# A displaced 5x5 convolution behind a group norm: group sums as four lane tiles inside the first stage, one lane evicted by VectorE, matrices written in place

## The chip, the cores and the metric

One NeuronCore of a Trainium2 chip runs the kernel. The metric is the device time of one execution in microseconds (us), as the median of several runs. The engines are TensorE (PE; its weight loads are shown apart as PEld), VectorE (DVE), ScalarE (ACT), GpSimd (POOL) and SyncE (SP, which here only issues loads).

## The reference, cut to what matters

```python
x = x + conv(displace(group_norm(x)))      # x: (32, 384, 64, 64) float32

def group_norm(v, G=32, eps=1e-5):         # 12 channels of one image are a group
    return (g - mean(g)) / sqrt(var(g) + eps)

def conv(x, offset):                       # 48 positions, 8 channels each
    off_round = round(offset); sub = offset - off_round
    disp = displace(x, off_round)          # whole shifts per position, zeros shifted in
    d = field + sub                        # field: 5 x 5
    kernel = exp(-sum(d * d) / 0.5); kernel /= sum(kernel)   # one 5 x 5 kernel per position
    return depthwise_conv(disp, kernel)    # 384 channels
```

The 5x5 kernel is a product of a vertical and a horizontal Gaussian, so that shift and convolution of one channel are a product with a 64x64 matrix along the rows (`ay`) and one along the columns (`ax`).

## The kernel before

**Steps.** The channels are cut into 16 superblocks of 24 channels (3 positions each); within a superblock the 32 images are 16 steps of 2 images. There are 256 steps, named `t = 16 * c + s`; two steps are a pair, and there are 128 pairs. A step's data is a tile of 128 partitions by 6 x 256 numbers, 768 KB: the partitions are 4 lanes (channels) of 32, each of them 16 row blocks by 2 images. `xin` has 16 slots, one for each step of a superblock. Loads are issued by SyncE, two DMAs a step, as soon as the slot's store has landed; stores are issued by ScalarE, two DMAs a step, 2 steps behind (`BEHIND`, line 562).

**TensorE** (lines 592 to 674) goes through a loop whose body is one pair of steps (`two_steps`). Each step has a first stage, the y products (`y_product`, L604): 48 matmuls with 32 rows and 128 columns of weights (`norm`) and 128 moving columns (`ay`), four lanes side by side, into 4 PSUM banks; and a second stage, the x products (`x_products`, L615): 48 matmuls of 64 x 64 with 64 moving columns (`ax`), in the order of positions 2, 0, 1. In float32 every matmul is two weight loads and two matmul instructions. The even step uses PSUM half 0, the odd one half 1. The order in a pair is: y products of both steps, x products of the even step, the group sums (`sum_stats`, L596) for the pair two ahead, x products of the odd step, and the first third of the y products of the next pair (`begin_even`). The sums are one matmul of all 128 rows by 128 columns of `ones` with 36 moving columns, into a free piece of bank 3 of half 0. The last two pairs are written out behind the loop, without sums, and the very last without `begin_even`.

**VectorE** (lines 444 to 506) has for each step two additions of the result to `xin` (`add_x`: the third position's 512 numbers per partition first, L460, then 1024, L463). After the additions of an even step it reads the sums from PSUM (`sums`, L448), and after those of an odd step it does six `bn_stats` of 512 numbers (L441) for the two steps that are 8 (`AHEAD`) further on. Once a superblock it computes `t_msk` (`values`, L415, step 11), copies the next `ay` into place (`swap_rows`, L425, three copies ahead of the additions of step 14), and the next `ax` (`swap_columns`, L431, step 15).

**ScalarE** (lines 545 to 587) evicts each step's y product from PSUM (`copy_y`, L549, 1536 numbers per partition), issues the store, and normalises the first half of a step two ahead (L540). Once a superblock it squares, exponentiates, and fills the next `ay` (`fill_rows`, L530, two operations at step 13, into `next_ay`).

**GpSimd** (lines 242 to 325) normalises the other half (L294), makes the summands from the statistics (`make_summands`, L257 and L259, even steps) and the coefficients of the norm from the sums (`coefficients`, L274 to L285, odd steps), and once a superblock the distances and the next `ax` (`column_matrices`, L246, step 12, into `next_ax`).

All order between the engines is written out by hand as semaphores; each engine runs its list in order. TensorE's waits around the sums are:

```python
x_products(0)
if more:
    pe.wait_ge(summands_ready, one)
    pe.wait_ge(result0_ready, two)
    sum_stats()
pe.wait_ge(y_ready, two)
pe.sem_inc(x_started, 1)
x_products(1)
```

## Time and profile before

| | us |
|---|---|
| median of 3 runs | 1216.74 (1216.17 to 1218.03) |
| the profiled execution's own time | 1216.96 |
| its span in the trace | 1215.1 |
| PE busy | 1169.8 (96%) |
| PEld busy | 1127.1 (93%) |
| DVE busy | 995.5 (82%) |
| ACT busy | 697.5 (57%) |
| POOL busy | 660.9 (54%) |
| DMA | 403.01 MB, mean 332 GB/s |

The span is what the trace covers; the execution's own time has 1.9 us around it. A busy time is the sum over an engine's instructions. PE and PEld overlap, and a busy PE can still be slower than it might be, so the order and the starts of its phases in the timeline tell more than the share.

### The profile page before, as it was taken

To read this page: it belongs to the slowest core of one execution; us is meant where nothing else is said; L and a number is where in the kernel's file an instruction comes from. 1 tells how busy PE (TensorE), PEld (TensorE's weight loads), DVE (VectorE), ACT (ScalarE), POOL (GpSimd) and SP (SyncE) were. 2 spreads that over 40 slices of the span, in tenths; PEclk is the share of its full clock that TensorE was granted. 3 is DMA by queue.
4 is the path that set the end of the run, shared out by engine and by line. 5 is a ranking of instruction groups with operands and counts; after the bars stand their busy time and mean duration, and the time that the engine had idled before them with its cause. 6 is when DMAs were issued, how large, how long until landed. Compare 5 with 4: busy or idle time off the path is not lost.

```text
span 1215.1 us, 110760 instructions
## 1 busy us (share of the span) xinstructions
PE 1169.8 (96%) x49408; PEld 1127.1 (93%) x49408; DVE 995.5 (82%) x1530; ACT 697.5 (57%) x595; POOL 660.9 (54%) x1478
## 2 busy tenths in 40 slices
PE   2899999999999999999999999999999999999996
PEld 2899999999999999999999999999999999999996
DVE  7688788888888888788888878878888888878863
ACT  3455655656656565665665665565565566566553
POOL 5455555556565555655556555555655556564551
PEclk9899999999999999999999999999999999999999
DMA  9799999999999999999999999999999999999955
GB/s 311 248 321 334 347 347 344 343 342 345 344 338 342 346 349 345 341 344 345 346 341 346 344 336 349 340 347 344 341 347 339 347 339 350 343 344 343 336 182 185
DMA packets 409765, 403.01 MB, mean 332 GB/s; under 512 B 16528, under 2 KB 409744, under 8 KB 409744
## 3 DMA queue, kind: packets, MB, share of 16 engines
q1 hardware_dynamic: 204944, 201.41, 51.3%
q10 hardware_dynamic: 204800, 201.36, 49.4%
q8 instruction: 9, 0.15, 0.1%
q14 instruction: 12, 0.10, 0.0%
HBM read 201.38 MB, written 201.33 MB: 331 GB/s over the span
## 4 chain that ended last, share of the span: by engine, by line
PE 94%; DVE 2%; issue 2%; POOL 1%; DVEq 0%; POOLq 0%
PE ps L604 59%; PE ps L615 31%; PE ps L596 4%; DVE ay L425 1%; DVE xin L460 1%; POOL norm L294 0%; POOL t_int L232 0%; POOL t_full L238 0%; POOL grid_i L212 0%; DVE xin L463 0%; POOL var L281 0%; POOL rstd L283 0%; DVEq L423 0%; DVE sub L379 0%; DVE tap L341 0%
## 5 line engine op out<-in xcount | busy, mean ns | idle before, releaser
L604 PE MATMUL ps<-ay,norm 32*128 32x128 f32 x24576 | 728.0, 273 | 0.9 <-DVE both L448 0.3
L604 PEld LDWEIGHTS ps<-ay,norm 32*128 32x128 f32 x24576 | 704.6, 187 | 11.0 <-issue 0.7
L549 ACT ACTIVATE y<-ps 128x1536 f32<-128x1536 f32 x256 | 369.7, 1444 | 420.3 <-PE ps L604 420.1
L441 DVE BATCH_NORM_STATS2 stats<-xin 128x6 f32<-128x512 f32 x768 | 475.7, 689 | 0.1
L615 PE MATMUL ps<-ax,y 64*64 64x64 f32 x24576 | 419.4, 220 | 7.8 <-issue 7.6
L615 PEld LDWEIGHTS ps<-ax,y 64*64 64x64 f32 x24576 | 383.8, 135 | 29.6 <-issue 8.6
L294 POOL TENSOR_SCALAR norm<-xin,rstd,bias 128x768 f32<-128x768 f32 x256 | 264.1, 1032 | 211.1 <-PE ps L604 187.6
L463 DVE TENSOR_TENSOR xin<-ps,xin 128x1024 f32<-128x1024 f32 x256 | 312.7, 1222 | 45.7 <-PE ps L615 45.7
L540 ACT ACTIVATE norm<-xin,bias,rstd 128x768 f32<-128x768 f32 x256 | 262.9, 1028 | 73.8 <-issue 73.5
L460 DVE TENSOR_TENSOR xin<-ps,xin 128x512 f32<-128x512 f32 x256 | 175.6, 686 | 150.1 <-PE ps L615 150.1
L274 POOL TENSOR_TENSOR mean_sq<-both 128x4 f32<-128x4 f32 x128 | 25.5, 199 | 218.6 <-DVE both L448 198.2
L283 POOL TENSOR_TENSOR rstd<-var,mhalf 128x4 f32<-128x4 f32 x128 | 129.2, 1009 | 10.0
L596 PE MATMUL ps<-summands,ones 128*128 128x36 f32 x256 | 49.7, 278 | 30.6 <-POOL summands L259 23.2
L596 PEld LDWEIGHTS ps<-summands,ones 128*128 128x128 f32 x256 | 38.7, 190 | 41.3 <-issue 32.3
L259 POOL TENSOR_TENSOR summands<-stats 128x12 f32<-128x12 f32 x128 | 27.2, 213 | 20.9 <-POOL summands L257 20.8
L232 POOL TENSOR_TENSOR t_int<-grid,place 128x960 f32<-128x960 f32 x16 | 28.7, 1795 | 7.1 <-DVEq L395 7.0
L281 POOL TENSOR_TENSOR var<-spread,mean_sq 128x4 f32<-128x4 f32 x128 | 26.4, 206 | 10.0
L279 POOL TENSOR_TENSOR spread<-inner,both 128x4 f32<-128x4 f32 x128 | 25.8, 202 | 10.7
L530 ACT ACTIVATE next_ay<-t_msk,same 128x768 f32<-128x768 f32 x32 | 30.3, 1000 | 1.8 <-DVE t_msk L415 1.8
L276 POOL TENSOR_SCALAR inner<-both 128x4 f32<-128x4 f32 x128 | 25.4, 199 | 10.1
L285 POOL TENSOR_TENSOR bias<-minus_mean,rstd 128x4 f32<-128x4 f32 x128 | 25.5, 199 | 10.0
L238 POOL TENSOR_TENSOR t_full<-t_int,sub 128x960 f32<-128x960 f32 x16 | 28.7, 1797 | 0.1
(54 smaller groups left out, 188.2 us busy)
## 6 DMA issues: line engine op xcount, KB each, us to landing
xin<-in_x_dram SPq DMA_DIRECT2D x512, 384.0 KB, 5.6
out_dram<-xin ACTq DMA_DIRECT2D x512, 384.0 KB, 6.2
off<-in_L_conv_offset_dram SPq DMA_DIRECT2D x1, 48.0 KB, 3.4
```

The costliest lines, as they stand in the source:

```text
L232: pool.tensor_tensor(t_int[:], grid[:, None, :, :].to_broadcast([P, POS, KINDS, HW]), place[:, bass.ds(POS * c, POS), :].unsqueeze(3).to_b ...
L283: pool.tensor_tensor(rstd[:, v], var[:, v], mhalf[:, :], ALU.pow).then_inc(small, 1)
L294: pool.tensor_scalar(norm[:, s % 2, :, cols].rearrange("p r (q w) -> p q r w", w=HW), xin[:, s, QG:].rearrange("p q (r w) -> p q r w", w=H ...
L441: nc.vector.bn_stats(stats[:, s // PAIR % RING, s % PAIR, n, :], xin[:, s].rearrange("p (g q) f -> p q f g", g=GROUPS)[:, n]).then_inc(bn_ ...
L460: nc.vector.tensor_tensor(at, ps[:, s % 2, 2:4, 0:ROW], at, ALU.add).then_inc(result0_ready, 1)
L463: nc.vector.tensor_tensor(at, ps[:, s % 2, 0:2].rearrange("p h (k f) -> p h k f", k=2), at, ALU.add).then_inc(result1_ready, 1)
L530: nc.scalar.activation(next_ay[:].rearrange("p n r (m b) -> p n (r m) b", b=B)[:, :, :, part], t_msk[:, :, 0:R].rearrange("p n r m -> p n ...
L540: nc.scalar.activation(norm[:, s % 2, :, cols].rearrange("p r (q w) -> p q r w", w=HW), xin[:, s, 0:QG].rearrange("p q (r w) -> p q r w", ...
L549: nc.scalar.activation(y[:, v].rearrange("p k r a m -> p a (k r) m"), ps[:, v, :, 0:POS * P].rearrange("p a (n m) -> p a n m", m=32), ACT. ...
L596: nc.tensor.matmul(ps[:, 0, 3, SUMS], ones[:, :], summands[:].rearrange("p t n s -> p (t n s)"), start=True, stop=True).then_inc(stat_summ ...
L604: last = nc.tensor.matmul(ps[:, v, a, P * k:P * (k + 1)], norm[rows, v, r, P * k:P * (k + 1)], ay[rows, k, r, :], start=(r == 0), stop=(r ...
L615: last = nc.tensor.matmul(ps[outs, v, 2 * (k // 2) + h, at:at + HW], y[rows, v, k, r].rearrange("p a m -> p (a m)")[:, outs], ax[rows, k], ...
```

## The change

The sums become four matmuls, one for each lane of 32 partitions, each into its lane's PSUM bank, and move from between the x products into the even step's y products (behind position 1's). VectorE's reduction adds up the four banks as well; since position 1's x products overwrite those columns, the x products of the even step now wait for it. The reduction moves from behind the even step's additions to just ahead of the last of the six statistics, one pair further in the count, and waits for ScalarE's eviction of the even step. In odd steps ScalarE evicts three lanes and VectorE the fourth (`copy_last_lane`). ScalarE and GpSimd write `ay` and `ax` in place, once the last use of the old ones is over (step 15): six ScalarE operations of 256 numbers in place of two of 768; `next_ay`, `next_ax`, `swap_rows` and `swap_columns` go. TensorE's loop covers all 128 pairs, all with sums and with `begin_even` (a first third of y products of a pair that doesn't exist, behind the last pair; ScalarE raises the semaphores for it). On GpSimd both small groups now run in odd steps, coefficients first and then summands.

```diff
@@ GpSimd
             def column_matrices(c):
                 pool.wait_ge(made, c + 1)
                 if c is not 0:
-                    pool.wait_ge(ax_ready, STEPS * c)
-                pool.tensor_tensor(next_ax[:], t_msk[:, :, R, :],
+                    pool.wait_ge(x_done, ADDS * STEPS * c)
+                pool.tensor_tensor(ax[:], t_msk[:, :, R, :],
...
-                                   ALU.mult).then_inc(next_ax_ready, 1)
+                                   ALU.mult).then_inc(ax_ready, STEPS)
...
+            make_summands(2, 2)
...
-                if not (tail and s // PAIR + LEAD >= STEPS // PAIR):
-                    if s % PAIR == 0:
-                        make_summands(p + LEAD, (s // PAIR + LEAD) % RING)
+                if s % PAIR == 1:
+                    if not (tail and s // PAIR + LEAD >= STEPS // PAIR):
+                        coefficients(p + LEAD, (s // PAIR + LEAD) % 2)
+                    if not (tail and s // PAIR + LEAD + 1 >= STEPS // PAIR):
+                        make_summands(p + LEAD + 1, (s // PAIR + LEAD + 1) % RING)
                     else:
-                        coefficients(p + LEAD, (s // PAIR + LEAD) % 2)
+
+                        pool.engine_nop().then_inc(summands_ready, PAIR)
...
-                    if s == 12:
+                    if s == STEPS - 1:
                         column_matrices(c + 1)
@@ VectorE
-            def sums(pair, v, early=False, read=False):
+            def sums(pair, v, early=False, read=False, evicted=None):
...
+                if evicted is not None:
+                    dve.wait_ge(y_ready, evicted)
                 ready = nc.vector.tensor_reduce(
                     both[:, v].rearrange("p (t g) f -> p t (g f)", t=PAIR),
-                    ps[:, 0, 3, SUMS].rearrange("p (t n e) -> p t e n", t=PAIR, n=CHUNKS), AX.X, ALU.add)
+                    ps[:, pair if early else 0, :, SUMS].rearrange("p a (t n e) -> p t e a n", t=PAIR, n=CHUNKS),
+                    AX.XY, ALU.add)
...
+            def copy_last_lane(t):
+                dve.wait_ge(y_done, t + 1)
+                nc.vector.tensor_copy(y[:, 1].rearrange("p k r a m -> p a (k r) m")[:, LANES - 1],
+                                      ps[:, 1, LANES - 1, 0:POS * P].rearrange("p (n m) -> p n m", m=32)
+                                      ).then_inc(last_lane_ready, PAIR)
...
+            def pair_statistics(c, s, p, reduced):
+
+                for f in (s, s + 1):
+                    for part in range(CHUNKS):
+                        if reduced and f > s and part == CHUNKS - 1:
+                            reduced()
+                        statistics(c + f // STEPS, f % STEPS, part, p if f == s and part == 0 else None)
+
+            pair_statistics(0, 4, None, None)
+            pair_statistics(0, 6, None, lambda: sums(LEAD, LEAD % 2, read=True, evicted=1))
 
             def step(c, s, head, tail):
                 t, p = STEPS * c + s, STEPS // PAIR * c + s // PAIR
-                if s == STEPS - PAIR and not tail:
-                    swap_rows(c + 1)
+                if s % PAIR == 0:
+                    copy_last_lane(t + 1)
                 for part in range(ADDS):
                     add_x(t, s, part)
...
+                            sums(p + LEAD + 1, (s // PAIR + LEAD + 1) % 2, read=True, evicted=t + PAIR)
@@ ScalarE
-            def fill_rows(c, part):
-                if part == 0:
+            def fill_rows(c, k):
+                if k == 0:
                     act.wait_ge(made, c + 1)
...
+                for part in range(B):
+                    filled_k = nc.scalar.activation(ay[:, k].rearrange("p r (m b) -> p (r m) b", b=B)[:, :, part],
+                                                    t_msk[:, k, 0:R].rearrange("p r m -> p (r m)"), ACT.Identity,
+                                                    scale=same[:, part:part + 1])
+                filled_k.then_inc(mats_ready[k], STEPS)
...
             def copy_y(t, v, first):
+
+                lanes = LANES - v
...
+                nc.scalar.activation(y[:, v].rearrange("p k r a m -> p a (k r) m")[:, 0:lanes],
+                                     ps[:, v, 0:lanes, 0:POS * P].rearrange("p a (n m) -> p a n m", m=32),
                                      ACT.Copy).then_inc(y_ready, 1)
...
+                if s == STEPS - 1 and not tail:
+                    for k in range(POS):
+                        fill_rows(c + 1, k)
@@ TensorE
-            def sum_stats():
-                nc.tensor.matmul(ps[:, 0, 3, SUMS], ones[:, :],
-                                 summands[:].rearrange("p t n s -> p (t n s)"),
-                                 start=True, stop=True).then_inc(stat_summed, 1)
+            def sum_stats(v):
+                for a in range(LANES):
+                    rows = slice(32 * a, 32 * a + 32)
+                    last = nc.tensor.matmul(ps[:, v, a, SUMS], ones[rows, :],
+                                            summands[rows].rearrange("p t n s -> p (t n s)"), start=True, stop=True)
+                last.then_inc(stat_summed, 1)
...
                 pe.wait_ge(mats_ready[1], one)
                 y_product(1, 0)
+                pe.wait_ge(summands_ready, one)
+                sum_stats(0)
                 pe.wait_ge(mats_ready[2], one)
                 y_product(2, 0)
...
                 pe.wait_ge(ax_ready, one)
+                pe.wait_ge(sums_ready, one)
                 pe.wait_ge(y_ready, one)
                 pe.sem_inc(x_started, 1)
                 x_products(0)
-                if more:
-                    pe.wait_ge(summands_ready, one)
-                    pe.wait_ge(result0_ready, two)
-                    sum_stats()
+                pe.wait_ge(last_lane_ready, one)
                 pe.wait_ge(y_ready, two)
                 pe.sem_inc(x_started, 1)
                 x_products(1)
-                if not last:
-
-                    pe.wait_ge(result0_ready, two)
-                    pe.wait_ge(result1_ready, two)
-                    if more:
-                        pe.wait_ge(sums_ready, one)
-                    begin_even(three)
+
+                pe.wait_ge(result0_ready, two)
+                pe.wait_ge(result1_ready, two)
+                begin_even(three)
 
             pe.wait_ge(filled, FILLS)
             pe.wait_ge(first_summands, 1)
-            sum_stats()
+            sum_stats(0)
             pe.wait_ge(first_sums, 1)
+            begin_even(1)
             pe.wait_ge(first_summands, 2)
-            sum_stats()
-            pe.wait_ge(first_sums, 2)
-            begin_even(1)
-            with pe.Fori(1, PAIR * (PAIRS - LEAD) + 1, PAIR) as one:
+            sum_stats(1)
+            with pe.Fori(1, TOTAL + 1, PAIR) as one:
                 two_steps(one)
-            for p in range(PAIRS - LEAD, PAIRS):
-                two_steps(PAIR * p + 1, more=False, last=p == PAIRS - 1)
```

## Rows read from the trace of the kernel before

**Rows 1.** Two stretches: us, busy PE, PEld, DVE, ACT, POOL, PEclk, DMA share, GB/s.

```profile
56.00:60.00 4.00, 4.00 (x178) 3.75 (x173) 2.41 (x5) 3.80 (x4) 2.77 (x5) 1.00 1.08 378
...
600.00:700.00 100.00, 98.97 (x4224) 95.48 (x4218) 85.44 (x131) 58.89 (x51) 55.81 (x125) 1.00 1.05 345
```

**Rows 2.** Waits of TensorE, the repeated one: us in total, times, longest us.

```profile
PE ps L596 <- DVE xin L460: 7.0, 14, 0.5
```

**Rows 3.** Timeline of one pair of steps: start us, us, engine, instruction, count, idle before.

```profile
601.30 5.47 PEld L604 LDWEIGHTS ps<-ay,norm 32*128 32x128 f32 x192
...
604.42 1.45 ACT L549 ACTIVATE y<-ps 128x1536 f32<-128x1536 f32 x1 [3.63 <-PE ps L604]
...
606.20 1.15 DVE L415 SCALAR_TENSOR_TENSOR t_msk<-t_isq,t_exp 128x960 f32<-128x960 f32 x1
606.89 1.49 PEld L615 LDWEIGHTS ps<-ax,y 64*64 64x64 f32 x96
...
607.12 1.44 ACT L549 ACTIVATE y<-ps 128x1536 f32<-128x1536 f32 x1
...
608.47 0.30 PEld L596 LDWEIGHTS ps<-summands,ones 128*128 128x128 f32 x2
...
608.59 1.22 DVE L463 TENSOR_TENSOR xin<-ps,xin 128x1024 f32<-128x1024 f32 x1 [0.24 <-PE ps L615]
608.81 1.49 PEld L615 LDWEIGHTS ps<-ax,y 64*64 64x64 f32 x96
...
608.82 1.03 ACT L540 ACTIVATE norm<-xin,bias,rstd 128x768 f32<-128x768 f32 x1 [0.26 <-issue]
...
610.37 5.47 PEld L604 LDWEIGHTS ps<-ay,norm 32*128 32x128 f32 x192
```

**Rows 4.** Groups of instructions, shapes apart: busy us, mean ns, idle before, releaser.

```profile
L604 PEld LDWEIGHTS ps<-ay,norm 32*128 32x128 f32 x24576 | 704.6, 187 | 11.0 <-issue 0.7 <-DVE both L448 0.5
...
L615 PEld LDWEIGHTS ps<-ax,y 64*64 64x64 f32 x24576 | 383.8, 135 | 29.6 <-issue 8.6
...
L596 PEld LDWEIGHTS ps<-summands,ones 128*128 128x128 f32 x256 | 38.7, 190 | 41.3 <-issue 32.3
...
L523 ACT ACTIVATE t_exp<-t_fsq 128x960 f32<-128x960 f32 x16 | 15.8, 988 | 0.0
```

**Rows 5.** Timeline around a superblock's matrix copies.

```profile
616.24 1.10 DVE L425 COPY ay<-next_ay 128x512 f32<-128x512 f32 x3 [0.88 <-PE ps L604]
...
616.27 1.76 POOL L294 TENSOR_SCALAR norm<-xin,rstd,bias 128x768 f32<-128x768 f32 x1 [1.14 <-PE ps L604]
...
617.25 0.68 DVE L460 TENSOR_TENSOR xin<-ps,xin 128x512 f32<-128x512 f32 x1
...
618.05 0.30 PEld L596 LDWEIGHTS ps<-summands,ones 128*128 128x128 f32 x2 [0.60 <-issue]
```

**Rows 6.** Timeline of the next pair: VectorE and GpSimd.

```profile
610.00 0.20 POOL L274 TENSOR_TENSOR mean_sq<-both 128x4 f32<-128x4 f32 x1 [0.92 <-DVE both L448]
...
611.65 3.72 DVE L441 BATCH_NORM_STATS2 stats<-xin 128x6 f32<-128x512 f32 x6
...
612.36 0.20 POOL L285 TENSOR_TENSOR bias<-minus_mean,rstd 128x4 f32<-128x4 f32 x1
...
613.59 0.99 POOL L294 TENSOR_SCALAR norm<-xin,rstd,bias 128x768 f32<-128x768 f32 x1 [1.02 <-PE ps L604]
...
614.91 0.22 POOL L259 TENSOR_TENSOR summands<-stats 128x12 f32<-128x12 f32 x1 [0.15 <-POOL summands L257]
```

**Rows 7.** Timeline of the last pairs, weight loads.

```profile
1196.70 0.79 PEld L615 LDWEIGHTS ps<-ax,y 64*64 64x64 f32 x48 [1.55 <-issue]
...
1208.02 0.89 PEld L615 LDWEIGHTS ps<-ax,y 64*64 64x64 f32 x51 [1.78 <-issue]
```

**Rows 8.** DMA issues: KB each, median us from issue to landing.

```profile
xin<-in_x_dram SPq DMA_DIRECT2D x512, 384.0 KB, 5.6
out_dram<-xin ACTq DMA_DIRECT2D x512, 384.0 KB, 6.2
```

More of the change, by code:

```diff
@@ L148, in displaced_conv @@
         y_ready = sem("y_ready")
+        last_lane_ready = sem("last_lane_ready")
         x_started = sem("x_started")
@@ L556, in _ @@
             act.wait_ge(filled, FILLS)
-            for part in range(B):
-                fill_rows(0, part)
-            for s in range(PAIR):
-                normalise(s, s, 0, True)
+            fill_rows(0, 0)
+            normalise(0, 0, 0, True)
+            fill_rows(0, 1)
+            fill_rows(0, 2)
+            normalise(1, 1, 0, True)
             def store(c, s, t):
@@ L624, in begin_even, with two_steps @@
                 y_product(0, 0)
-            def two_steps(one, more=True, last=False):
-                two, three = one + 1, one + 2
-                if not isinstance(one, int):
-                    two, three = pe.snap(two), pe.snap(three)
+            def two_steps(one):
+                two, three = pe.snap(one + 1), pe.snap(one + 2)
                 pe.wait_ge(norm1_ready, one)
```

58 lines of the change are left out of this document (16 added, 42 removed).

## The prediction

> **What bounds the kernel now.** I read the busy times of whole stretches first: in 100 us of the middle TensorE is busy for 98.97, at full granted clock [rows 1]. The waits of its matmuls hold one repeated stall only, 14 waits, 7.0 us, for VectorE's addition [rows 2]. So TensorE's own sequence sets the period, and I read the timeline of one pair of steps for what that sequence consists of [rows 3]. By first weight loads, the pair starts its y products at 601.30, its even step's x products at 606.89, the sums at 608.47, the odd step's x products at 608.81, and the next pair starts at 610.37: a period of 9.07 us. The 128 pairs at 9.07 and the 14 stalls make 1168 of the 1215.1 us; the rest is head (loads, clock, code) and tail. I then read when the other engines start relative to the first x load (call it A = 606.89), since the change removes time from TensorE and their chains come next: the odd y eviction at A+0.23, the larger part of the even step's addition at A+1.70.
>
> **The sums leave the x products.** An x phase has 96 weight loads in 1.49 us of which the last takes 0.135 [rows 3, 4], so its last load starts 1.355 after its first, four loads every 0.057. The last load before the sums is at 608.245 and the first after them at 608.81: 0.565 us in which the sums own only two loads. Without them the next group follows after 0.057, so 0.51 us goes.
>
> **The sums enter the y products.** Four products of 32 rows by 128 columns, 36 columns moving, in eight loads. Two rows bound them. If a product costs by its moving columns, it is 36/128 of a y product: y loads take (5.47 - 0.187)/191 = 27.7 ns each [rows 3, 4], eight 0.22, and 36/128 of it 0.06. If the load sets the pace, it is 0.22. The present sums decide this: their two loads end 0.30 after the first began and each takes 0.19 [rows 3, 4], so the second follows the first by 0.11 although only 36 columns move; that is the pace of a group of four y loads (4 x 27.7 = 111 ns). I take 0.22. The tile shape is that of the y products on both sides, so I add no change of shape. If the four lanes did not overlap it would be 8 x 0.11 = 0.88, the upper bound. A to A, the y part grows from 5.59 to 5.81.
>
> **What is late next.** The odd x products could now start at A+1.41. Their operand is the odd eviction. ScalarE begins it at A+0.23; for 1536 columns it takes 1.44, and 960 columns take 0.988 [rows 3, 4], so 0.79 ns a column; with 1152 columns left, 1.14. From an engine's end to TensorE's load I take 0.12: the addition at 617.25 ends at 617.94 and the sums start at 618.05 [rows 5]. The odd x products then start at A+0.23+1.14+0.12 = A+1.49, last load A+2.85, and the next y after the usual 0.20, A+3.05. The second limit is the even addition: its second part starts at A+1.70, takes 1.22, so y may start at A+3.04. Both say that the x part shrinks from 3.48 to about 3.05, of the 3.48 - 0.51 = 2.97 it could be. VectorE's copy of the last lane is 384 columns: at the pace of the ay copies, which read SBUF (three of 512 in 1.10 [rows 5]), 0.3; at the rate of the additions, which read PSUM (0.68 for 512, 1.22 for 1024 [rows 3, 5]), 0.55. It reads PSUM, so 0.55; it starts near A+0.3 and is ready before A+1.0, ahead of A+1.49. **Period: 5.81 + 3.05 = 8.86 against 9.07, 0.21 a pair, over 127 pairs 26 us saved.**
>
> **VectorE's cycle.** Ahead of the copy stand, from A, the additions of both steps, behind which the statistics start now at 611.65, A+4.76, with the old reduction (0.1 apart) in between: A+4.66. Then five statistics at 0.61 each (a sixth of 3.72, a little less as they overlap): A+7.7 [rows 3, 6]. The new reduction waits for ScalarE's even eviction, which ends 4.57 after the y start now (604.42 + 1.45 - 601.30), plus 0.22, so it starts at A+7.8 to A+7.9. It reads 144 columns for 36: from 0.2 (its time if the columns cost nothing) to four times that, 0.8; at the additions' ns per column 0.3, which I take. TensorE needs it at A+8.86 less 0.12: slack 0.5, and none lost at 0.8 either. The last statistic ends near A+8.8 and the next copy starts at A+9.15. Nothing is lost in an ordinary pair, but in the pair with the values operation (1.15 us, step 11) VectorE comes about 0.7 late: copy from A+1.0, additions by A+3.4, next y at A+3.5. I price that at 0.45 for 15 superblocks: 7 us lost.
>
> **Matrices in place.** The three ay copies of 616.24 hold the addition until 617.25, and the sums wait for it until 618.05 [rows 5]: 0.5 each time by the waits [rows 2], at 15 changes of superblock (14 are put down to the addition) 8 us, all removed. Their replacement is six ScalarE operations of 256 columns right behind the odd eviction and its store issues: ScalarE is free for them at about A+1.93 (the norm behind them starts at 608.82 now [rows 3]), two at some 0.45 spaced 0.4 make the first matrix ready at A+2.9, just ahead of A+3.05; the others are needed 0.9 and 2.0 later. Cost nothing, covered by 0.1; without that cover some 0.2 x 15 = 3 us. The column matrix is one GpSimd operation (0.5) behind the last x product and a whole y part ahead of its use: nothing.
>
> **GpSimd's order.** Odd norm from A+0.31 (1.0), coefficients 2.56 (610.00 to 612.56), summands 0.6 (from the norm's end at 614.58 to 615.13) [rows 6]: ready at A+4.5, with 0.12 A+4.6. TensorE asks for them 64 loads into y, A+3.05+1.77 = A+4.82. Slack 0.2, so nothing, but thin. The DMA issues stay in their places on SP and ScalarE.
>
> **Head and tail.** In the last pairs, whose code is written out behind the loop, TensorE's loads stop with nothing to wait for (1.55 us before 1196.70, 1.78 before 1208.02, and shorter ones) [rows 7]. One loop to the end has no such code: about 4 us saved, after paying 0.22 for two more sums. The extra y product at the end runs beside the last store. In the head the first y starts earlier, but then waits in the first sums for pair 2's summands, whose statistics VectorE has not done; I put the head at +1, between -3 (the first y at 22 instead of 24.8) and +5 (all of the wait for VectorE's two more steps of statistics, 3.7, and a cold clock behind it).
>
> **Sum**, against the profiled execution's own 1216.96 (span 1215.1): -26 - 8 + 7 - 4 + 1 = -30 to -31, **1186**. The median, 1216.74, is 0.2 from it.
>
> **Rivals.** (a) *The limits at A+3.05 are softer than they look*: ScalarE's start or the addition comes a little earlier and the values pair loses nothing. Period towards 8.78, 10 more saved, 7 not lost: 1169 to 1176. For: both limits are within 0.1 of the free pace. (b) *A chain with thin slack binds each pair*: GpSimd's summands (slack 0.2). While the ay copies ran, a norm took 1.76 instead of 0.99 [rows 5, 6]; if the lane copy blocks GpSimd for 0.35 to 0.55, the sums wait 0.15 to 0.35, at the lower 19 in 127 pairs: about 1205. The Trainium skill (VectorE: DVE Perf Modes, section Why PSUM operands drop a tier) says that an operation with a PSUM operand cannot use both SBUF read ports; by that the lane copy would not block GpSimd as the ay copies did, and the period stays at 8.86. No row here shows a copy from PSUM on VectorE. (c) *DMA*: 345 GB/s now, 3.146 MB a pair; at 8.86 that is 355. A stretch of 4 us reached 378 [rows 1]. If 345 were all, TensorE would gain only what loads are early. A store lands 6.2 after issue and the slot's next load 5.6 after its own [rows 8]. The store of step t is issued during step t + 2, the statistics read the slot at the end of step t + 8: six steps, 27 us and more, less 12, leaves some 15 to 18 us that can be used up: 1199 to 1202. The Trainium skill (DMA: Bandwidth & Descriptors, section Specifications) gives some 358 GB/s as HBM limit per core; by that a pair takes at least 8.79, and the stretch at 378 is above it. (d) *Slower*: the four lane products do not overlap. Place: the sums in the y part; price 0.88 instead of 0.22, +0.66 x 127 = 84 us: 1270. It decides from a price of 0.22 + 30/127 = 0.46 on. Against: y products of the same shape advance four per 111 ns. (e) *The change doesn't take the gaps away*: the 0.565 is not drained shape changes but sequencer waits that reappear at the moved waits (sums and lane flags before the x products). Then 0.22 is paid and 0.2 to 0.3 saved: about 1212 to 1219.
>
> **Numbers.** Forecast 50%, (a) 15, (b) 14, (c) 9, (d) 5, (e) 7. The time is the forecast's, 1186. Range 1171 to 1206: most of (a), (b), (c) and the bounds of the copy (0.2 a pair is 25 us, the widest). A measurement tells 0.2% (2.4 us) from no change. Faster: 50 + 15 + 14 + 9 + 2 = 0.90; same 0.04; slower 0.06.
>
> **What would show it.** Right: y starts 8.8 to 8.9 apart, no 128-row matmul, eight loads of the sum's line within 0.22 and not followed by a gap; x loads 192 with one gap of about 0.1; evictions of 1.14 and 1.44 in turn; no copy of ay; a late y start only after the values operation; no code gaps in the tail. Wrong: TensorE waiting for summands (b), the load queue landing just before its statistics (c), sum loads 0.11 apart one by one (d), gaps around waits with their writers long done (e).

## The result, and the profile after

The changed kernel takes 1221.22 us (median of 8 runs, 1219.82 to 1222.21) against 1217.95 for the kernel before beside it: 1.0026 times as long, with a 95% interval of 1.0016 to 1.0036. The prediction, 1186 with a range of 1171 to 1206 and 0.06 for slower, is wrong in its sign. The profiled execution has a span of 1218.0 us, 2.9 more than before.

The page of the changed kernel: span, busy times, and the groups that the change made or touched (instructions | busy us, mean ns | idle before, releaser).

```profile
span 1218.0 us, 112847 instructions
PE 1153.6 (95%) x50224; PEld 1121.0 (92%) x50224; DVE 1064.5 (87%) x1594; ACT 665.5 (55%) x659; POOL 659.1 (54%) x1478
...
L619 PEld LDWEIGHTS ps<-ay,norm 32*128 32x128 f32 x24608 | 722.1, 188 | 48.8 <-issue 32.3
L556 ACT ACTIVATE y<-ps 128x1536 f32<-128x1536 f32 (+1 forms) x256 | 328.4, 1283 | 414.3 <-PE ps L619 414.2
...
L450 DVE COPY y<-ps 128x384 f32<-128x384 f32 x128 | 71.2, 557 | 32.8 <-PE ps L619 32.8
L439 DVE TENSOR_REDUCE both<-ps 128x12 f32<-128x144 f32 x128 | 39.4, 308 | 67.1 <-ACT y L556 64.7
...
L611 PEld LDWEIGHTS ps<-summands,ones 32*128 32x128 f32 x1040 | 45.6, 189 | 19.7 <-issue 16.1
```

The first line to compare is that of the y loads: the idle time ahead of them is 48.8 us, where it was 11.0 [rows 4]. The new pieces have the sizes that were predicted: the lane copy 0.557 (0.55), the reduction 0.308 (0.3).

In the middle 100 us TensorE is now idle for 2.3, where it was idle for 1.0 [rows 1]:

```profile
600.00:700.00 100.00, 97.68 (x4288) 94.92 (x4284) 90.71 (x134) 56.70 (x59) 55.42 (x125) 1.00 1.04 342
```

The timeline of one pair of the changed kernel, to be laid beside [rows 3]: start, duration, engine, instruction, idle before and releaser.

```profile
659.06 1.91 PEld L619 LDWEIGHTS ps<-ay,norm 32*128 32x128 f32 x64 [0.39 <-ACT norm L545]
660.85 0.35 PEld L611 LDWEIGHTS ps<-summands,ones 32*128 32x128 f32 x8
661.07 3.70 PEld L619 LDWEIGHTS ps<-ay,norm 32*128 32x128 f32 x128
...
663.97 0.31 DVE L439 TENSOR_REDUCE both<-ps 128x12 f32<-128x144 f32 x1 [0.50 <-ACT y L556]
...
664.89 3.06 PEld L630 LDWEIGHTS ps<-ax,y 64*64 64x64 f32 x192
...
665.09 0.56 DVE L450 COPY y<-ps 128x384 f32<-128x384 f32 x1 [0.20 <-PE ps L619]
...
665.11 1.11 ACT L556 ACTIVATE y<-ps 128x1152 f32<-128x1152 f32 x1
665.19 0.98 POOL L291 TENSOR_SCALAR norm<-xin,rstd,bias 128x768 f32<-128x768 f32 x1 [1.69 <-PE ps L619]
...
666.58 1.23 DVE L461 TENSOR_TENSOR xin<-ps,xin 128x1024 f32<-128x1024 f32 x1 [0.24 <-PE ps L630]
...
668.13 1.01 PEld L619 LDWEIGHTS ps<-ay,norm 32*128 32x128 f32 x32 [0.18 <-issue]
```

The y part is 664.89 - 659.06 = 5.83, and the sums take 661.07 - 660.85 = 0.22 of it. All 192 x loads run through in 3.06, where two groups with the sums between took 608.81 + 1.49 - 606.89 = 3.41. Both are as predicted. What is not is the last line: the even addition starts at A+1.69 (A = 664.89, the first x load) and ends at 667.81, and the next y load comes at 668.13, 0.32 later, instead of 0.12. The x part is 3.24, not 3.05, and the period 9.07 where before had 9.07 as well.

The next view is the list of TensorE's waits (us in total, times, longest us), of which [rows 2] was the one repeated row before:

```profile
PE ps L619 <- issue: 16.3, 72, 0.3
PE ps L619 <- ACT norm L545: 10.8, 23, 5.1
PE ps L619 <- DVE xin L461: 5.6, 18, 0.4
```

Now 113 waits are listed ahead of y products. The list gives three different releasers for one and the same place in the program, and in 72 of the 113 none ("issue"); that ScalarE's norm is the cause turned out false for 22 of its 23 rows (below).

**Where the 2.9 us are.** By the first y loads of pairs 2, 126 and 127 (counted from 0):

| | before | after | difference | predicted |
|---|---|---|---|---|
| up to pair 2 | 52.45 | 51.96 | -0.5 | +1 |
| pairs 2 to 125 (124 periods) | 1134.59 | 1141.29 | +6.7 | -27 |
| mean period in these | 9.150 | 9.204 | +0.054 | -0.22 |
| pair 126, pair 127 and the end | 28.05 | 24.77 | -3.3 | -4 |

The tail came as predicted and the head within 1.5 us; the middle missed by 34 us. (The head can't be read closer than 2 to 3 us: from 44 to 48 us the mean granted clock was 0.88 of full in the trace of before, 1.00 in that of the changed kernel, and 0.56 in that of wait_last below, whose pair 2 starts at 54.29.) The mean of before, 9.150, also shows that the pair at 9.07 from which the prediction worked is not the average one.

### The profile page after: what moved, and what is told of

The parts are those of the page before. It is cut to its first block, busy times and chain, and to the rows that moved or that the text cites. A ratio compares the mean times of both kernels' runs of the same rounds, so it can differ in the third digit from the quotient of the medians.

```text
span 1218.0 us, 112847 instructions
## 1 busy us (share of the span) xinstructions
PE 1153.6 (95%) x50224; PEld 1121.0 (92%) x50224; DVE 1064.5 (87%) x1594; ACT 665.5 (55%) x659; POOL 659.1 (54%) x1478
## 4 chain that ended last, share of the span: by engine, by line
PE 93%; issue 3%; ACTq 1%; ACT 0%; DVE 0%; DVEq 0%
PE ps L619 60%; PE ps L630 31%; PE ps L611 2%; ACTq L574 1%; ACT norm L545 0%; DVE xin L461 0%; DVEq L54 0%; ACT ay L534 0%; DVE xin L458 0%; ACTq L555 0%; ACT y L556 0%; ACTq L542 0%; ACTq L180 0%; ACTq L532 0%; ACTq L572 0%
## 5 line engine op out<-in xcount | busy, mean ns | idle before, releaser
L619 PE MATMUL ps<-ay,norm 32*128 32x128 f32 x24608 | 756.0, 275 | 34.8 <-issue 16.3
L619 PEld LDWEIGHTS ps<-ay,norm 32*128 32x128 f32 x24608 | 722.1, 188 | 48.8 <-issue 32.3
L556 ACT ACTIVATE y<-ps 128x1536 f32<-128x1536 f32 (+1 forms) x256 | 328.4, 1283 | 414.3 <-PE ps L619 414.2
L429 DVE BATCH_NORM_STATS2 stats<-xin 128x6 f32<-128x512 f32 x768 | 486.9, 690 | 0.0
L630 PE MATMUL ps<-ax,y 64*64 64x64 f32 x24576 | 405.4, 221 | 5.1 <-issue 4.4
L461 DVE TENSOR_TENSOR xin<-ps,xin 128x1024 f32<-128x1024 f32 x256 | 312.0, 1219 | 41.6 <-PE ps L630 41.6
L450 DVE COPY y<-ps 128x384 f32<-128x384 f32 x128 | 71.2, 557 | 32.8 <-PE ps L619 32.8
L439 DVE TENSOR_REDUCE both<-ps 128x12 f32<-128x144 f32 x128 | 39.4, 308 | 67.1 <-ACT y L556 64.7
L611 PE MATMUL ps<-summands,ones 32*128 32x36 f32 x1040 | 46.8, 237 | 19.2 <-POOL summands L256 19.2
L611 PEld LDWEIGHTS ps<-summands,ones 32*128 32x128 f32 x1040 | 45.6, 189 | 19.7 <-issue 16.1
L534 ACT ACTIVATE ay<-t_msk,same 128x256 f32<-128x256 f32 x96 | 41.2, 519 | 11.5 <-issue 8.9
```

The lines of the kernel that those rows point to most:

```text
L429: nc.vector.bn_stats(stats[:, s // PAIR % RING, s % PAIR, n, :], xin[:, s].rearrange("p (g q) f -> p q f g", g=GROUPS)[:, n]).then_inc(bn_ ...
L450: nc.vector.tensor_copy(y[:, 1].rearrange("p k r a m -> p a (k r) m")[:, LANES - 1], ps[:, 1, LANES - 1, 0:POS * P].rearrange("p (n m) -> ...
L461: nc.vector.tensor_tensor(at, ps[:, s % 2, 0:2].rearrange("p h (k f) -> p h k f", k=2), at, ALU.add).then_inc(result1_ready, 1)
L534: filled_k = nc.scalar.activation(ay[:, k].rearrange("p r (m b) -> p (r m) b", b=B)[:, :, part], t_msk[:, k, 0:R].rearrange("p r m -> p (r ...
L556: nc.scalar.activation(y[:, v].rearrange("p k r a m -> p a (k r) m")[:, 0:lanes], ps[:, v, 0:lanes, 0:POS * P].rearrange("p a (n m) -> p a ...
L611: last = nc.tensor.matmul(ps[:, v, a, SUMS], ones[rows, :], summands[rows].rearrange("p t n s -> p (t n s)"), start=True, stop=True)
```

## The experiments

Two theories stood after the first reading. **W**: TensorE's own way through the waits ahead of the y products. The result waits (for VectorE's additions) stand first in the program and the waits for norm and matrix behind them, so when the addition ends, the sequencer (the part of TensorE that goes through its instructions and waits in order) still has work to do. **E**: ScalarE, or the lane copy that delays VectorE, is late, as the list of waits says. A third, **S**, asks if the old sums ever cost the pair anything.

### wait_last: the two result waits directly ahead of the first y product

```diff
-            def begin_even(number):
+            def begin_even(number, results=None):
                 pe.wait_ge(norm0_ready, number)
                 pe.wait_ge(mats_ready[0], number)
+                if results is not None:
+                    pe.wait_ge(result0_ready, results)
+                    pe.wait_ge(result1_ready, results)
                 y_product(0, 0)
...
-                pe.wait_ge(result0_ready, two)
-                pe.wait_ge(result1_ready, two)
-                begin_even(three)
+                begin_even(three, two)
```

> The changed kernel with TensorE's two waits on VectorE's additions placed last ahead of the next pair's y products, behind the waits for the norm and the matrix. Theory 1 (ring): each pair is bound by the end of the even step's additions plus the path from there to TensorE's first load, 0.33 us in the changed kernel's trace, of which some 0.15 are the register step and the wait that stand between: 0.15 to 0.2 less a pair, 19 to 25 us, 1196 to 1202. Theory 2 (ScalarE's norm holds the y products, as the list of waits names it) and theory 3 (VectorE's load as a whole): no change, 1219 to 1223.

Measured: 1197.97 us, 0.9839 (0.9822 to 0.9855) of before, 23 us faster than the changed kernel with the same work in it. Its timeline:

```profile
646.85 3.07 PEld L630 LDWEIGHTS ps<-ax,y 64*64 64x64 f32 x192
...
648.72 1.23 DVE L461 TENSOR_TENSOR xin<-ps,xin 128x1024 f32<-128x1024 f32 x1 [0.41 <-PE ps L630]
...
650.06 1.91 PEld L619 LDWEIGHTS ps<-ay,norm 32*128 32x128 f32 x64
```

From the addition's end (649.95) to the y load it is 0.11: the prediction's 0.12 holds where the wait that ends last is the last one in the program. The rows of ScalarE's norm and of the addition are gone from the list of waits (the only row of the norm left is one of 5.1 us in the head), so W holds, ScalarE is not what holds the y start back, and the list's 22 shorter waits for ScalarE were a wrong attribution. In the changed kernel the records of TensorE's sequencer show what lies in the 0.32: the wait for the addition of 1024 numbers passes at 667.85, a register instruction follows at 667.97, the wait for the matrix `ay` at 668.06 although that is raised once a superblock only and was long there, and the first load, which carries the norm's wait, at 668.13. In wait_last the register instruction has passed at 649.73, before the addition ends, and one wait stands between its end and the load.

In this pair the addition starts at A+1.87 instead of A+1.70, and the mean period is 9.009, still more than the forecast's. That is the second open piece.

### before_wait_last: the same on the kernel before

```diff
-                    pe.wait_ge(result0_ready, two)
-                    pe.wait_ge(result1_ready, two)
                     if more:
                         pe.wait_ge(sums_ready, one)
-                    begin_even(three)
+                    begin_even(three, two)
```

> The kernel before with TensorE's waits on the additions placed last ahead of the next y products. Theory 1 (in the kernel before the additions' path ended 0 to 0.1 short of TensorE's own, and past it in the jittered pairs only): the period falls from 9.09 to 9.065 at most, 2 to 5 us, 1213 to 1216. If the path of waits bound the kernel before as it binds the changed one: 0.2 a pair, 1190 to 1195.

Measured: 1217.92 us, 1.0002 (0.9993 to 1.0012). The edit is worth nothing here, not even the 2 to 5 us expected, and the timeline of this kernel says why it tells less than it should:

```profile
599.90 1.22 DVE L463 TENSOR_TENSOR xin<-ps,xin 128x1024 f32<-128x1024 f32 x1 [0.36 <-PE ps L615]
...
601.04 0.18 DVE L448 TENSOR_REDUCE both<-ps 128x12 f32<-128x36 f32 x1
...
601.57 5.48 PEld L604 LDWEIGHTS ps<-ay,norm 32*128 32x128 f32 x192
```

In the kernel before the old reduction follows the even addition on VectorE, and TensorE waits for it as well. It ends at 601.22, 0.10 behind the addition, and is the wait that ends last. The edit moved the waits for the additions behind the others and left this one in front: the sequencer passes it, on the register step, at 601.26 and has two more waits behind it (601.39 and 601.50). So y starts 0.35 after the reduction, where it is 0.33 without the edit (next section). The run shows that the additions' own waits don't bind there; the order of the reduction's wait was not tried on the kernel before. Little could have come of it: in the traces of both kernels y follows TensorE's last x load by 0.20 in the median pair, the shortest time that is found there, and in the pairs 10 to 124 of before all that goes beyond it adds up to 1.4 us.

### before_no_sums: the kernel before without the sums in its pairs

```diff
                     pe.wait_ge(result0_ready, two)
-                    sum_stats()
+                    pe.sem_inc(stat_summed, 1)
```

> The kernel before whose loop leaves out the matmuls of the group sums (the coefficients stay those of the first pairs). Theory 1 (the sums stood in the shadow of the even additions): y cannot start before the additions' end plus 0.41, A+3.34 to A+3.5, against A+3.47 to A+3.54 now: about 0.1 a pair and most of the 15 copy stalls, 1198 to 1204. The prediction's reading (the sums own 0.51 us, only the eviction stands behind them, y at A+3.29): 0.18 a pair and the stalls, 1185 to 1190.

Measured: 1213.05 us, 0.9956 (0.9939 to 0.9973): 4.7 us less than the kernel before beside it (1217.73). The prediction's first term says that 0.51 leaves TensorE's sequence, of which 0.43 a pair (3.48 to 3.05) could be had: over 127 pairs 55 us. Only a tenth of that came, and both expectations, 1198 to 1204 and 1185 to 1190, missed as well. The timeline says why:

```profile
605.52 1.49 PEld L615 LDWEIGHTS ps<-ax,y 64*64 64x64 f32 x96
605.75 1.43 ACT L549 ACTIVATE y<-ps 128x1536 f32<-128x1536 f32 x1
...
607.22 1.23 DVE L463 TENSOR_TENSOR xin<-ps,xin 128x1024 f32<-128x1024 f32 x1 [0.24 <-PE ps L615]
607.29 1.52 PEld L615 LDWEIGHTS ps<-ax,y 64*64 64x64 f32 x96 [0.28 <-issue]
...
608.88 5.51 PEld L604 LDWEIGHTS ps<-ay,norm 32*128 32x128 f32 x192
```

The even addition ends at 608.45 and y starts at 608.88, 0.43 later, A+3.36. (The reduction still runs; only the products are gone.) The odd x products wait for ScalarE's eviction until A+1.77 and end near the place where the additions' path ends. Both other chains already ended within 0.15 of the place at which y starts with the sums; in the median pair, whose addition starts at A+1.82 and so later than in this one, y comes at A+3.47 without the sums as with them. So S is settled: the old sums stood in the shadow of the even addition and of the odd eviction, and cost the pair next to nothing. (The y part is 0.03 longer in this run, 5.63 against 5.60, for which no run shows a cause.)

That shadow can be seen in the kernel before, in a pair whose addition starts late; it is a row that the prediction didn't look for:

```profile
717.02 1.49 PEld L615 LDWEIGHTS ps<-ax,y 64*64 64x64 f32 x96
...
718.91 1.22 DVE L463 TENSOR_TENSOR xin<-ps,xin 128x1024 f32<-128x1024 f32 x1 [0.44 <-PE ps L615]
...
720.05 0.18 DVE L448 TENSOR_REDUCE both<-ps 128x12 f32<-128x36 f32 x1
...
720.56 5.48 PEld L604 LDWEIGHTS ps<-ay,norm 32*128 32x128 f32 x192
```

The addition starts at A+1.89 and ends at 720.13, the reduction ends at 720.23, and y starts at 720.56, which is A+3.54. From the reduction it is 0.33, from the addition 0.43 (0.42 is the least in any pair). So in a pair with the addition at A+1.70 this path ends at 1.70 + 1.22 + 0.42 = A+3.34, 0.13 ahead of TensorE's own A+3.47, and in the pairs with a late addition it bound already.

### in_place_only: the matrices in place, on the kernel before

```diff
             def column_matrices(c):
...
-                    pool.wait_ge(ax_ready, STEPS * c)
-                pool.tensor_tensor(next_ax[:], t_msk[:, :, R, :],
+                    pool.wait_ge(x_done, ADDS * STEPS * c)
+                pool.tensor_tensor(ax[:], t_msk[:, :, R, :],
...
-            def swap_rows(c):
...
-            def swap_columns(c):
...
-            def fill_rows(c, part):
+            def fill_rows(c, k):
...
+                if s == STEPS - 1 and not tail:
+                    for k in range(POS):
+                        fill_rows(c + 1, k)
```

> The kernel before with this one part of the change: matrices written in place, no copies of them on VectorE. All theories: 15 stalls of 0.52 us go, nothing else moves: 1209 to 1211. If ScalarE's six operations hold the first y products of a superblock, up to 3 us of it come back: 1213.

Measured: 1207.66 us, 0.9915 (0.9898 to 0.9931): 10.1 us faster than the kernel before beside it (1217.73), where 8 had been put down for it. At a change of superblock the sums now follow the x loads at once, without the 0.60 of [rows 5]:

```profile
612.48 1.49 PEld L592 LDWEIGHTS ps<-ax,y 64*64 64x64 f32 x96
...
614.05 0.30 PEld L573 LDWEIGHTS ps<-summands,ones 128*128 128x128 f32 x2
```

This part of the change works by itself; the rest of it must then cost what this brings and more.

### scalar_evicts_all, and the same on wait_last

```diff
                 if s % PAIR == 0:
-                    copy_last_lane(t + 1)
...
-                lanes = LANES - v
+                lanes = LANES
...
-                pe.wait_ge(last_lane_ready, one)
                 pe.wait_ge(y_ready, two)
```

> The changed kernel with ScalarE evicting all four lanes in odd steps and no copy on VectorE. Theory 1 (ring): the odd x products start at A+1.73 instead of A+1.46 and would let y start at A+3.3, while the additions allow it at A+3.25 to A+3.43: at most 0.05 a pair, against 0.2 saved in the 15 pairs with the values operation: 1216 to 1225. By the prediction's step (the eviction is the limit) 0.3 more a pair: 1250 to 1260. Theory 3 (VectorE's load): 0.4 to 0.5 a pair less, 1165 to 1180.

Measured: 1222.86 us, 1.0038 (1.0024 to 1.0053), 1.6 more than with the lane copy, which is within the noise. So by itself the copy brings nothing. Whether it delays the additions this run alone can't tell, since ScalarE's longer eviction could hide the gain; the second run can.

> wait_last with ScalarE evicting all four lanes (as scalar_evicts_all, but with the waits last). Theory 1: the lane copy on VectorE was worth nothing while the additions' path bound, and is worth something now: the odd x products start at A+1.77 instead of A+1.46, y at A+3.34 instead of A+3.19: 0.15 a pair, less some 3 us in the pairs with the values operation: 1210 to 1218. If it is worth nothing here either: 1196 to 1200.

Measured: 1221.34 us, 1.003 (1.0019 to 1.0041). On wait_last the same edit costs 23.4 us, more than the 12 to 20 expected. The even addition starts at A+1.82 in the median pair with the copy (wait_last) and without it, so the copy doesn't delay it in an ordinary pair, and with that the rest of E falls. One pair of the run:

```profile
604.04 1.49 PEld L628 LDWEIGHTS ps<-ax,y 64*64 64x64 f32 x96
604.26 1.44 ACT L554 ACTIVATE y<-ps 128x1536 f32<-128x1536 f32 x1
...
605.82 1.52 PEld L628 LDWEIGHTS ps<-ax,y 64*64 64x64 f32 x96 [0.28 <-issue]
...
607.40 1.90 PEld L617 LDWEIGHTS ps<-ay,norm 32*128 32x128 f32 x64
```

The eviction of four lanes ends at 605.70, the odd x products start at 605.82, A+1.78, and y at A+3.36. Two chains end at nearly the same place: by ScalarE A+3.36, by the additions with the changed kernel's order of waits A+3.24 in the pairs whose addition starts at A+1.70 and A+3.38 in the median one. Taking one away uncovers the other:

| | four lanes by ScalarE | lane copy |
|---|---|---|
| result waits first | 1222.86 | 1221.22 |
| result waits last | 1221.34 | 1197.97 |

Each edit alone is worth 1.5 us, less than the 2.4 that a measurement can tell from nothing; both together are worth 25.

### small_loads: wait_last with a sixth of the load traffic

```diff
-            def load(c, s):
+            def load(c, s, q=Q):
                 for b in range(B):
-                    sync.dma_start(xin[b:P:B, s], x_t[s, b, c]).then_inc(loaded[s], 16)
+                    sync.dma_start(xin[b:P:B, s, 0:q], x_t[s, b, c][:, 0:q]).then_inc(loaded[s], 16)
...
-                    load(c, s)
+                    load(c, s, 1)
```

> wait_last whose loads from the second superblock on fetch one sixth of each tile (the rest of a slot keeps older results, so the output differs). Open question: from pair 6 on the semaphore of the even step's last x product comes 0 to 0.2 us later than in pairs 2 to 5 (0.26 behind its matmul's start there), which makes the period 9.0 instead of 8.86. If the load on the DMA engines is behind it: period back to 8.86 to 8.9, 1178 to 1184. If not: 1196 to 1200. A kernel bound by loads would fall below 1175.

Measured: 1184.99 us, 0.9731 (0.9715 to 0.9747): 13.0 us less than wait_last, and the median period is 8.859, the 8.86 of the prediction. No wait for a load shows in wait_last, so this is not the bandwidth as such. The windows of the middle (us, busy PE, PEld, DVE, ACT, POOL, PEclk, DMA share, GB/s), of wait_last and of small_loads:

```profile
600.00:700.00 100.00, 99.53 (x4358) 96.95 (x4356) 92.03 (x137) 58.21 (x60) 56.28 (x126) 1.00 1.05 349
```

```profile
600.00:700.00 100.00, 99.85 (x4399) 97.42 (x4396) 92.59 (x137) 57.35 (x59) 57.55 (x128) 1.00 0.64 203
```

and one pair of small_loads:

```profile
604.65 3.00 PEld L630 LDWEIGHTS ps<-ax,y 64*64 64x64 f32 x192
...
606.35 1.23 DVE L461 TENSOR_TENSOR xin<-ps,xin 128x1024 f32<-128x1024 f32 x1 [0.24 <-PE ps L630]
...
607.72 1.89 PEld L619 LDWEIGHTS ps<-ay,norm 32*128 32x128 f32 x64
```

The addition starts at A+1.70 in 101 of 115 pairs (10 to 124); the other 14 are those behind a values operation. With full loads (wait_last) it does so in 34 of the 115; most of the rest start up to 0.2 later, in step with the moment at which TensorE's product counts as done: its semaphore comes 0.26 after the start of the last even x product in all 115 pairs of small_loads, and 0.23 to 0.47 after it in wait_last. TensorE's own pace has a part in it: the last x load starts at A+2.80 in the median pair of small_loads and at A+2.95 in that of wait_last, and y follows it by the shortest time, 0.20, in 61 of the 115 pairs of wait_last, so that in these the x loads bind and not the addition. By what mechanism the transfers delay either stays open. Nor is their rate enough for it: in sums_x_ordered (below) 355 GB/s flow, and the addition starts at A+1.70 in 96 of the 115 pairs.

### sums_twice: the sums of wait_last issued a second time

```diff
                 pe.wait_ge(summands_ready, one)
+                sum_stats(0, False)
                 sum_stats(0)
```

> wait_last with the four lane products of the sums done twice in the y part. Theory 1 (the y part lies wholly on the path): 0.22 a pair more, 28 us, 1224 to 1228. If part of it were covered by other work: less than 20 us. If the lanes did not overlap (rival d of the prediction): 80 us.

Measured: 1224.86 us, 1.0064 (1.0047 to 1.008), 26.9 more than wait_last. Eight loads at 0.22 over 127 pairs are 28. So what stands inside the y products is paid in full, and the prediction's 0.22 is right. The new place has no shadow; the old one lay almost wholly in one.

### sums_x_shape: the sums as four 64x64 products ahead of the odd x products

The sums leave the y products, and the lanes' sums are replaced by four products of the x products' own shape; VectorE adds up two banks behind the first part of the odd additions, and GpSimd's small groups go back to the order of the kernel before.

```diff
-            def sum_stats(v):
-                for a in range(LANES):
-                    rows = slice(32 * a, 32 * a + 32)
-                    last = nc.tensor.matmul(ps[:, v, a, SUMS], ones[rows, :],
+            def sum_stats():
+                for h, m in ((0, 0), (1, 0), (0, 1), (1, 1)):
+                    rows, outs = slice(64 * h, 64 * h + 64), slice(64 * m, 64 * m + 64)
+                    last = nc.tensor.matmul(ps[outs, 1, 2 + h, SUMS], ones[rows, outs],
...
-                pe.wait_ge(sums_ready, one)
                 pe.wait_ge(y_ready, one)
                 pe.sem_inc(x_started, 1)
                 x_products(0)
+                pe.wait_ge(summands_ready, one)
                 pe.wait_ge(last_lane_ready, one)
                 pe.wait_ge(y_ready, two)
                 pe.sem_inc(x_started, 1)
+                sum_stats()
                 x_products(1)
```

> wait_last with the sums as four 64 x 64 products, the shape of the x products, at the start of the odd step's x products, into free columns of banks 2 and 3 of the odd half; VectorE reads them behind the first of the odd additions, GpSimd's small groups in the order of the kernel before. Theory 1 (ring of y products, even x products, even addition, 0.1 for the wait): the 0.23 of the sums leave the y part (5.59) and their 0.12 lie in the additions' shadow: y at A+3.1 to A+3.2, period 8.72 to 8.8, 1167 to 1178. If TensorE's own loads bind instead: 5.59 + 3.08 + the same, still under 1180. If VectorE's work as a whole bound wait_last: no gain, 1196 to 1200.

Measured: 1179.89 us, 0.9693 (0.9677 to 0.9709), 18 less than wait_last and 2 above the range expected. The same kernel ran once more:

> Placeholder for the order of the waits ahead of the odd x products: not changed here, so the same as sums_x_shape, 1180.

Measured: 1179.87 us in one run, the same time. The timeline, the odd step's part:

```profile
625.17 1.49 PEld L622 LDWEIGHTS ps<-ax,y 64*64 64x64 f32 x96
...
625.50 1.11 ACT L548 ACTIVATE y<-ps 128x1152 f32<-128x1152 f32 x1
...
626.84 0.24 PEld L603 LDWEIGHTS ps<-summands,ones 64*64 64x64 f32 x8 [0.18 <-issue]
626.95 1.53 PEld L622 LDWEIGHTS ps<-ax,y 64*64 64x64 f32 x96
```

The sums cost 626.95 - 626.84 = 0.11, half of what they cost as lane tiles. ScalarE's eviction, though, ends at 626.61 and the sums' first load comes 0.23 later, with another 0.18 "issue": the pattern of the y start again, a wait that ends last and has a step behind it.

### sums_x_ordered: the eviction's wait brought to the end

```diff
                 pe.wait_ge(summands_ready, one)
+                pe.sem_inc(x_started, 1)
                 pe.wait_ge(last_lane_ready, one)
                 pe.wait_ge(y_ready, two)
```

No engine waits for `x_started`. The added increment ahead of the two eviction waits keeps them, in the compiled program, behind the wait for the summands (602.79 and 602.94 in the pair below).

> sums_x_shape with the wait for the summands put in front, so that the waits for the two evictions stand last ahead of the odd step's first loads (in sums_x_shape the compiled order puts the eviction's wait first and another wait step behind it: 0.21 us from the eviction's semaphore to the first load, 0.06 in the changed kernel). Theory 1: the odd x products start 0.1 to 0.15 earlier, y at A+3.12 to A+3.2: 10 to 16 us less, 1164 to 1170. If the eviction does not hold them: no change, 1180.

Measured: 1170.07 us, 0.9609 (0.9593 to 0.9626). It is 4.2% faster than the changed kernel, 3.9% faster than the kernel before, and the fastest of the study. Two pairs of it:

```profile
601.59 1.49 PEld L622 LDWEIGHTS ps<-ax,y 64*64 64x64 f32 x96
...
603.15 0.24 PEld L603 LDWEIGHTS ps<-summands,ones 64*64 64x64 f32 x8
603.26 1.52 PEld L622 LDWEIGHTS ps<-ax,y 64*64 64x64 f32 x96
...
604.86 5.51 PEld L611 LDWEIGHTS ps<-ay,norm 32*128 32x128 f32 x192
...
610.49 1.49 PEld L622 LDWEIGHTS ps<-ax,y 64*64 64x64 f32 x96
```

The eviction in this pair (601.98, 1.11) ends at 603.09 and the sums start 0.06 later. The x part is 604.86 - 601.59 = 3.27 and the y part 610.49 - 604.86 = 5.63: 8.90 here, 8.81 on the mean of 124. In 108 of the 115 pairs y follows the last x load by the shortest time, 0.20: TensorE's own sequence binds again. In the middle it has no idle time left:

```profile
600.00:700.00 100.00, 100.00 (x4455) 97.45 (x4454) 90.77 (x138) 58.30 (x57) 59.68 (x130) 1.00 1.05 355
```

## Why the prediction was wrong

**Its reading of what bounds the kernel** took from TensorE's 98.97% busy [rows 1] and the single repeated wait [rows 2] that TensorE's own sequence sets the period. It does, but the next chain, which the prediction put 0.43 away, was 0.13 away: A+3.34 against A+3.47. The list of waits doesn't show a chain that ends just ahead of the one that binds, and in pairs with a late addition it bound already without a row there.

**The step that failed** is "What is late next": "From an engine's end to TensorE's load I take 0.12". The 0.12 came from [rows 5], a wait ahead of the sums with nothing behind it. At the y products the same way has a register step and one more wait, that for the matrix, behind it and takes 0.32 (in the kernel before 0.33 from the reduction, which itself ends 0.10 behind the addition). wait_last shows 0.11 there as soon as that is gone. With it y starts at A+1.70+1.22+0.32 = A+3.24, not A+3.04, and the term "0.43 less in the x part" becomes 0.24 in an ordinary pair, of which the sums in the y part take 0.22 back.

**The second term that was mis-sized** is the start of the even addition, A+1.70, read from one pair. The mean is A+1.83 in the changed kernel and 1.78 before. In the kernel before most of these delays fell inside TensorE's own 3.47; in the changed kernel y follows the addition's end by 0.32 to 0.33 in 102 of the 115 pairs, and the delays are on the path. With the two terms put right the changed kernel's period comes out as 5.82 + 1.83 + 1.22 + 0.32 = 9.19, where 9.204 was measured.

By pairs 10 to 124, medians, with A the first even x load:

| | addition starts | y from its end, least | next y starts | y part, mean |
|---|---|---|---|---|
| predicted | A+1.70 | 0.12 | A+3.05 | 5.81 |
| before | A+1.77 | 0.42 | A+3.47 | 5.60 |
| the changed kernel | A+1.83 | 0.32 | A+3.38 | 5.83 |
| wait_last | A+1.82 | 0.11 | A+3.19 | 5.82 |
| small_loads | A+1.70 | 0.11 | A+3.04 | 5.82 |

The last row has the times that were predicted. The two steps make up 36 us in the middle: 0.195 a pair between the changed kernel and wait_last (9.204 to 9.009), 24 us over 124 periods; and 0.098 between wait_last and small_loads (9.009 to 8.911), 12 us. That is the 34 that were missed and 2 to 3 more, because the saving was taken off before's mean, which gives 8.93; 8.86 with 0.45 more in 15 of 127 pairs is a mean of 8.91, and small_loads has that. That it meets it so closely is luck: the pair behind a values operation costs 0.33 there (9.19 against 8.86) and not 0.45, while two others in a superblock cost 0.05 to 0.07 that were not foreseen.

**Point by point.**
- Sums in the y part, 0.22: right, and shown twice (y part 5.82, sums_twice).
- Sums out of the x products, 0.51: right as time of TensorE's sequence, but worth 5 us alone and not 0.43 a pair.
- Rival (a), softer limits: no; in none of the pairs 10 to 124 of the changed kernel does y start before A+3.24.
- Odd x products at A+1.49: they start at A+1.41 in the median pair (1.39 to 1.76); the eviction begins at A+0.23, as predicted, and takes 1.11 (predicted 1.14), and the first load came 0.06 after such an eviction in sums_x_ordered and not 0.12.
- Lane copy, reduction: right in size. The Trainium skill (VectorE: DVE Perf Modes, section Why PSUM operands drop a tier), by which an operation with a PSUM operand cannot use both SBUF read ports, agrees with the trace: GpSimd's norm took 0.98 beside the copy, as without it. Rival (b) does not occur: no repeated wait for the summands.
- Matrices in place: 8 predicted, 10 measured by themselves. Tail: 4 predicted, 3.3 measured. Head: +1 predicted, -0.5 measured up to pair 2, with the clock of the head as said above.
- Rival (c), the transfers: no wait for a load appears. sums_x_ordered carries the same loads and stores in the shorter time:

```profile
100.00:1100.00 1000.00, 999.39 (x44480) 974.51 (x44476) 915.83 (x1376) 586.64 (x585) 576.75 (x1291) 1.00 1.06 357
```

  357 GB/s over 1000 us with TensorE idle for 0.6 of them. The Trainium skill (DMA: Bandwidth & Descriptors, section Specifications) names some 358 GB/s as HBM limit per core. The trace stands at that figure over 1000 us and shows no wait from it, and the 4 us of [rows 1] at 378 are above it; whether it would hold a still shorter period back was not tried.
- Rival (d): no; the eight loads take 0.22 together. Rival (e), 7%, came nearest in time (1212 to 1219) and in form, "gaps around waits": its place was wrong, though. The gaps did not reappear at the moved waits ahead of the x products, which are passed without one, but at waits that the change didn't touch and that had been in the shadow. Its condition was never worked out for that place.

The range failed for the same reason: its ends were made of unknown prices of new operations, while the price that decided was that of an old wait, and was in the trace.

## What to carry to other kernels

Before pricing a removal on the busiest engine, compute for several pairs when the other chain into the next phase ends, with the latency measured at that very wait and the spread of its start: the gain is no more than that distance. Put the wait that ends last directly ahead of the instruction it guards, and waits that are long fulfilled ahead of it. If an edit is worth nothing and two chains end at nearly the same time, try it together with the edit on the other one: here two edits of 1.5 us each gave 25.

## What the runs showed of the hardware that was not expected

- A wait on TensorE that is already fulfilled is not free when it stands behind the one that ends last: from the end of VectorE's addition to the first load it takes 0.11 us with the wait directly ahead of the product, and 0.32 with a register step and one more wait behind it; at the eviction's wait ahead of the odd step 0.23 (sums_x_shape) and 0.06 (sums_x_ordered). Moving the wait was worth 23 us at the first place and 10 at the second.
- The moment at which VectorE can start on an x product's result wanders by up to 0.2 us in wait_last, where transfers run at 349 GB/s, and, outside the pair behind a values operation, not in small_loads at 203 GB/s, with TensorE at full granted clock in both (median period 9.00 against 8.86). In sums_x_ordered, at 355 GB/s, it hardly does (96 of 115 pairs at A+1.70), so the rate of the transfers alone doesn't decide it.
- The same sums cost TensorE 0.51 as one 128-row product between x products, 0.22 as four lane tiles among the y products and 0.11 as four 64x64 tiles among the x products. The Trainium skill (TensorEngine Tiling (Array Packing), section Key Properties) says that a change of tiling mode drains TensorE, without a time for it. The trace agrees in that the two forms that keep their neighbours' shape have no gap around them; the price of the change of mode was not measured by itself.
